# Query weight and half of the key weight loaded as float32 and cast by VectorE, with the prologue in a new order

## The chip, the cores and the metric

The kernel runs on all 8 cores of one Trainium2 chip. Each core works on its own 4,096 tokens, and no core waits for another. The metric is the device time of one execution in microseconds, that of the slowest core. Engines are named as in the profile: PE is TensorE (matrix products), PEld its weight loads, DVE is VectorE, ACT is ScalarE, POOL is GpSimd, and SP is SyncE, which only issues transfers (SPq).

## The reference

The input is x, 2 sequences of 16,384 tokens with 1,024 features. One layer is computed:

```
xn  = layernorm(x)
q, k, v = xn @ w_q + b_q, xn @ w_k + b_k, xn @ w_v + b_v      # 16 heads of 64
att = softmax over the 7 neighbouring tokens of q.k / 8, times v
t   = clip(round(w_ffn / s), -1, 1) * s,  s = max(mean |w_ffn|, 1e-5)
out = x + (att @ w_o + b_o) + xn @ t.T
```

All five weights are 1,024 x 1,024 in float32. The matrix products are made in bfloat16.

## The kernel before

A core reads its rows of x in 33 tiles of 128 tokens. Tokens are further grouped in 34 windows of 122 queries and 128 keys, and four windows make a block. A block of transposed, normalised inputs lies in one of three buffers `xnt`. The output comes in 32 tiles of 128 tokens.

A program in Python writes out, by hand and in order, one list of instructions for each engine (`Queues`). `q.do` appends an instruction, `q.dma` a transfer, and `q.need` a wait for a named result. Each engine works through its list strictly in order, so an instruction that waits holds up everything behind it on that engine. Transfers that SyncE issues go through one queue and follow each other there; GpSimd's go through another, and the two share the 16 DMA engines.

Each x tile goes through these steps: `x_load` (SyncE), `stats` (VectorE), `rstd` (two small instructions on ScalarE, a logarithm and an exponential), `normalise` (VectorE), and then a transpose. In the prologue (tiles 0 to 7, blocks 0 and 1) TensorE transposes and ScalarE copies the result (`xn_by_pe`); later a DMA does it (`xn_by_dma`).

A job on TensorE (`q_job`, `k_job`, `v_job`) is eight matmuls into one of three banks of `p_p`. ScalarE empties the bank (in the main loop VectorE does so for k), and a fourth job has to wait until the first bank is empty. `q_job(b, c)` and `k_job(b, c)` make 128 of the 1,024 output columns for block b, and c below 4 needs half 0 of the weight, the rest half 1.

For each window i and each half hf of the heads there follow: `scores` (TensorE), `mask_max` (VectorE: the mask addition, which frees the scores' bank, and then the row maximum), `exps` (ScalarE), `weights` (VectorE: reciprocal and product), `e_transpose` (a DMA), `att_v` (TensorE) and `att_evict` (ScalarE).

The feed-forward weight `wft` is loaded as float32 into memory that is otherwise used later (`wf_load`: the buffers of xr, the third xnt, et, att). VectorE sums the absolute values of its eight pieces (`wf_abs`); `wf_scale` forms the scale with one small matmul; `wf_tern` makes a ternary piece with two VectorE instructions, and all eight are wanted by the first feed-forward product.

The four attention weights are loaded by GpSimd and cast to bfloat16 on the way (`weight_load`): one transfer for 512 rows of a half, 1 MB read and 512 KB written. Waits in the lists of GpSimd and SyncE ("gates") set when they start:

- half 0 of wq in two pieces, after tiles 1 and 2 of x have landed
- x tile 4, behind half 0 of wq, in SyncE's list, and the tiles 5 to 7 behind it
- half 1 of wq and both halves of wk after tile 6 of x
- the eight pieces of wft after half 0 of wk, and x tiles 8 to 10 behind them
- wv and wo after the sixth piece of wft

The order of TensorE's jobs in the prologue is: q of block 0, c 0 to 3; q of block 1, c 0 to 3; the other q jobs; k of block 0, c 0 to 7; scores of window 0, half 0; two k jobs of block 1; `wf_scale`; scores of half 1; the other k jobs; v of window 0. Then the main loop begins: step s computes the scores and v of window s + 1 and finishes window s. In steps 4 and on it also makes the q and k jobs of the next block.

Of the kernel before, what the change touches and what calls it, by code (L numbers as in the profile page):

```python
# [91 lines left out]
def build_program():  # L92
# [13 lines left out]
    slots = (["cm", "cb", "ci", "bo"] + [f"{n}{k}" for n in ("wq", "wk", "wv", "wo") for k in range(2)] + [f"x{k}" for k in range(5)] + [f"r{k}" for k in range(NR)]  # L106
# [3 lines left out]
    with contextlib.ExitStack() as st:  # L110
# [52 lines left out]
        def weight_load(n, half, parts=(0, 1)):  # L163
            cols = slice(512 * half, 512 * half + 512)
            for k in parts:
                q.dma("gpsimd", f"{n}{half}", lambda e, k=k: e.dma_start(
                    w_b[n][:, 4 * k * H:(4 * k + 4) * H].rearrange("p (c n) -> p c n", c=4, n=H)[:, :, cols],
                    w_h[n][512 * k:512 * k + 512, cols].rearrange("(c p) n -> p c n", c=4, p=128)),
                    ("w", n, half))
# [109 lines left out]
        def q_job(b, c):  # L279
            n, bank = next_bank()  # L280
            m = TQ * nwin(b)
            q.need("tensor", ("w", "wq", c // 4), *[("xnt", b, r) for r in tiles_of(b)])
# [14 lines left out]
        def k_job(b, c, by="vector"):  # L297
            n, bank = next_bank()
            m = TQ * nwin(b) + KW - TQ
            q.need("tensor", ("w", "wk", c // 4), *[("xnt", b, r) for r in tiles_of(b)])  # L300
# [21 lines left out]
        def v_job(i, jh):  # L322
            b, w = divmod(i, BW)
            n, bank = next_bank()
            q.need("tensor", ("w", "wv", jh), *[("xnt", b, r) for r in tiles_of(b)])
# [131 lines left out]
        def o_proj(t):  # L457
            i = out_step(t)
            acc = p_out(t)
            q.need("tensor", ("w", "wo", 0), ("w", "wo", 1), ("att", i, 0))  # L460
# [67 lines left out]
        def wf_tern(j, k):  # L528
            up = w_b["wft"][:, k * H:(k + 1) * H]
            dn = brow[:, 512 * (j % 2):512 * (j % 2) + 512].bitcast(BF16)  # L530
            q.need("vector", "wthr")
# [9 lines left out]
        def bias_half(jh):  # L541
            n, bank = next_bank()
            q.need("tensor", ("w", "wo", jh), "bvb")
# [21 lines left out]
        q.need("gpsimd", ("x", 1))  # L565
        weight_load("wq", 0, (0,))
        q.need("gpsimd", ("x", 2))
        weight_load("wq", 0, (1,))
        q.need("sync", ("w", "wq", 0))
# [9 lines left out]
        bias_forms()  # L579
        normalise(3)  # L580
        for r in (5, 6, 7):
            x_load(r)
        q.need("gpsimd", ("x", 6))
        weight_load("wq", 1)
        weight_load("wk", 0)
        weight_load("wk", 1)
        xn_by_pe(3, 0, 1)
        for c in range(4):
            q_job(0, c)
            if c >= 1:  # L590
                stats(3 + c)
                rstd(3 + c)
                normalise(3 + c)
            if c >= 2:
                xn_by_pe(2 + c, 1)
        stats(7)
        rstd(7)
        normalise(7)
        xn_by_pe(6, 1)
        xn_by_pe(7, 1)  # L600
        q.need("sync", ("w", "wk", 0))
# [17 lines left out]
        for b, c in ([(1, c) for c in range(4)] + [(0, c) for c in range(4, 8)]  # L619
                     + [(1, c) for c in range(4, 8)]):  # L620
            q_job(b, c)
        for c in range(8):
            k_job(0, c, "scalar")
        scores(0, 0)
        mask_max(0, 0)
        k_job(1, 0, "scalar")
        k_job(1, 1, "scalar")
        wf_scale()
        some_terns(0, 2)
        scores(0, 1)  # L630
        mask_max(0, 1)
        some_terns(2, 4)
        for c in range(2, 8):
            k_job(1, c, "scalar")
            exps(0, (c - 2) // 3, ((0, 1), (2, 3, 4), (5, 6, 7))[(c - 2) % 3])
            if c == 5:
                weights(0, 0)
                some_terns(4, 6)
# [4 lines left out]
        weights(0, 1)  # L643
# [186 lines left out]
```

How the kernel before makes its waits and increments, by code:

```python
        def run(e, items):  # L754
            for f, sem, n in items:
                if f is None:
                    e.wait_ge(sems[sem], n)
                elif sem is None:
                    f(e)
                else:
                    f(e).then_inc(sems[sem], n)
```

## Time and profile before

| | |
|---|---|
| time, median of 3 runs | 695.19 us (694.86 to 695.31) |
| the profiled execution's own time | 696.35 us |
| its span, first to last instruction, slowest core (5) | 694.8 us |
| spans of the eight cores | 688.6 to 694.8 us |
| PE busy | 644.1 us, 93% |
| DVE busy | 434.4 us, 63% |
| ACT busy | 375.5 us, 54% |
| POOL busy | 88.6 us, 13% |

Busy time says how much work an engine has, not what sets the end. Views that show order are of more use here: the chain of waits follows the work that ended last back through what released each step; the timeline lists instructions with the idle time ahead of them and what ended it; the windows give busy time, the granted TensorE clock (1.00 is 2.4 GHz, 0.50 is 1.2 GHz) and the DMA engines' busy share for one stretch. All rows are of core 5.

### The profile page before, as it was taken

To read this page: it belongs to the slowest core of one execution; us is meant where nothing else is said; L and a number is where in the kernel's file an instruction comes from. 1 tells how busy PE (TensorE), PEld (TensorE's weight loads), DVE (VectorE), ACT (ScalarE), POOL (GpSimd) and SP (SyncE) were. 2 spreads that over 40 slices of the span, in tenths; PEclk is the share of its full clock that TensorE was granted. 3 is DMA by queue.
4 is the path that set the end of the run, shared out by engine and by line. 5 is a ranking of instruction groups with operands and counts; after the bars stand their busy time and mean duration, and the time that the engine had idled before them with its cause. 6 is when DMAs were issued, how large, how long until landed. Compare 5 with 4: busy or idle time off the path is not lost.

```text
span 694.8 us, 11677 instructions; the slowest of 8 cores (688.6 to 694.8 us)
## 1 busy us (share of the span) xinstructions
PE 644.1 (93%) x3890; PEld 299.8 (43%) x3890; DVE 434.4 (63%) x534; ACT 375.5 (54%) x1418; POOL 88.6 (13%) x52
## 2 busy tenths in 40 slices
PE   1669983999999999999999999999899999999996
PEld 1234431444444444444444444444344444455542
DVE  6225398686666667666665666666666755466663
ACT  3333465475555565656555555556556555555572
POOL 1202000221111111111111010011011111111110
PEclk9969996899999999999999999999999999999999
DMA  7699973768554444557563654544353442334423
GB/s 167 158 158 323 166 124 84 213 166 230 137 135 104 120 132 123 110 130 144 131 139 88 152 137 137 137 109 126 86 127 94 109 76 81 92 102 126 123 62 92
DMA packets 129947, 91.19 MB, mean 131 GB/s; under 512 B 107872, under 2 KB 116192, under 8 KB 129888
## 3 DMA queue, kind: packets, MB, share of 16 engines
q1 hardware_dynamic: 121440, 82.05, 45.9%
q0 software_dynamic: 8448, 8.39, 8.8%
q8 instruction: 32, 0.52, 0.3%
q14 instruction: 27, 0.22, 0.1%
HBM read 55.82 MB, written 16.78 MB: 104 GB/s over the span
## 4 chain that ended last, share of the span: by engine, by line
PE 83%; DVE 6%; DMA 4%; ACT 3%; issue 3%; DVEq 0%; SPq 0%; POOL 0%; ACTq 0%; POOLq 0%
PE p_p L284 16%; PE p_f L452 15%; PE p_p L302 15%; PE p_f L468 15%; PE p_p L327 15%; PE p_a L415 3%; PE p_s L355 3%; ACT sm L385 2%; DMA wq_b<-wq 1%; DVE sm L370 1%; DMA x<-x 1%; DMA sm<-x 1%; DVE bst L205 1%; DVE brow L534 1%; DVE wft_b L537 1%
## 5 line engine op out<-in xcount | busy, mean ns | idle before, releaser
L385 ACT ACTIVATE sm<-sm,nmx 122x128 f32<-122x128 f32 x544 | 210.9, 389 | 14.4 <-DVE nmx L377 14.4
L481 POOL TENSOR_TENSOR xr<-xr,brow 128x1024 f32<-128x1024 f32 x32 | 76.0, 2376 | 515.8 <-DMA xr<-x 452.3
L284 PE MATMUL p_p<-xnt,wq_b 128*128 128x488 bf16 (+1 forms) x576 | 129.2, 373 | 3.8 <-DMA wq_b<-wq 2.6
L327 PE MATMUL p_p<-wv_b,xnt 128*128 128x512 bf16 x544 | 124.5, 382 | 0.0
L302 PE MATMUL p_p<-xnt,wk_b 128*128 128x494 bf16 (+1 forms) x576 | 123.2, 361 | 0.0
L292 ACT ACTIVATE qt<-p_p,bq 128x488 bf16<-128x488 f32 (+1 forms) x72 | 46.5, 646 | 139.5 <-PE p_p L284 139.5
L452 PE MATMUL p_f<-wft_b,xnt 128*128 128x512 bf16 x496 | 114.7, 385 | 0.7 <-DVE xr L486 0.7
L468 PE MATMUL p_f<-wo_b,att 128*128 128x512 bf16 x496 | 113.2, 379 | 0.7 <-ACT att L432 0.7
L370 DVE TENSOR_TENSOR sm<-p_s,mk_sb 122x1024 f32<-122x1024 f32 x68 | 82.9, 1220 | 43.5 <-PE p_s L355 43.4
L385 ACT ACTIVATION_READ_ACCUMULATOR sm<-sm,nmx 122x1 f32 x544 | 102.4, 188 | 0.0
L340 ACT CAST v<-p_p 128x512 bf16<-128x512 f32 x68 | 39.0, 575 | 104.7 <-PE p_p L327 104.7
L398 DVE TENSOR_TENSOR en<-sm,rec 122x1024 bf16<-122x1024 f32 x68 | 83.3, 1226 | 11.6 <-DVE rec L392 11.4
L377 DVE TENSOR_REDUCE nmx<-sm 122x8 f32<-122x1024 f32 x68 | 83.0, 1220 | 7.4 <-DVE sm L370 0.5
L313 DVE TENSOR_SCALAR kt<-p_p,bias_sb 128x494 bf16<-128x494 f32 (+1 forms) x56 | 38.9, 695 | 77.4 <-PE p_p L302 77.4
L284 PEld LDWEIGHTS p_p<-xnt,wq_b 128*128 128x128 bf16 x576 | 57.7, 101 | 66.2 <-issue 13.1
L302 PEld LDWEIGHTS p_p<-xnt,wk_b 128*128 128x128 bf16 x576 | 56.2, 98 | 56.7
L327 PEld LDWEIGHTS p_p<-wv_b,xnt 128*128 128x128 bf16 x544 | 50.8, 98 | 60.8 <-issue 1.8
L452 PEld LDWEIGHTS p_f<-wft_b,xnt 128*128 128x128 bf16 x496 | 46.6, 99 | 56.4 <-issue 4.1
L468 PEld LDWEIGHTS p_f<-wo_b,att 128*128 128x128 bf16 x496 | 45.0, 98 | 56.6 <-issue 6.1
L392 DVE RECIPROCAL rec<-den 122x8 f32<-122x8 f32 x68 | 13.1, 192 | 66.4 <-ACT sm L385 66.4
L432 ACT ACTIVATE att<-p_a,wab 128x488 bf16<-128x488 f32 (+16 forms) x98 | 48.5, 524 | 11.1 <-PE p_a L415 10.9
L205 DVE BATCH_NORM_STATS2 bst<-x 128x6 f32<-128x512 f32 x62 | 39.6, 680 | 4.1 <-DMA x<-x 4.1
(62 smaller groups left out, 279.2 us busy)
## 6 DMA issues: line engine op xcount, KB each, us to landing
xr<-x SPq DMA_DIRECT2D x32, 512.0 KB, 4.7
x<-x SPq DMA_DIRECT2D x31, 512.0 KB, 4.5
out<-xr SPq DMA_DIRECT2D x31, 512.0 KB, 3.3
wq_b<-wq POOLq DMA_DIRECT2D x4, 512.0 KB, 9.1
wk_b<-wk POOLq DMA_DIRECT2D x4, 512.0 KB, 16.8
xr<-wft SPq DMA_DIRECT2D x4, 512.0 KB, 9.6
wv_b<-wv POOLq DMA_DIRECT2D x4, 512.0 KB, 16.0
wo_b<-wo POOLq DMA_DIRECT2D x4, 512.0 KB, 24.8
```

Of the source, the lines that this page charges most:

```text
L205: q.do("vector", lambda e, k=k: e.bn_stats(bs[:, 6 * k:6 * k + 6], xs[:, 512 * k:512 * k + 512]), ("bst", r, k))
L284: q.do("tensor", lambda e, k=k: e.matmul(bank[:, 0:m], w_b["wq"][:, k * H + 128 * c:k * H + 128 * c + 128], rows_of(b, k, BQ * b + 3, m), ...
L302: q.do("tensor", lambda e, k=k: e.matmul(bank[:, 0:m], w_b["wk"][:, k * H + 128 * c:k * H + 128 * c + 128], rows_of(b, k, BQ * b, m), star ...
L327: q.do("tensor", lambda e, k=k: e.matmul(bank, rows_of(b, k, TQ * i, KW), w_b["wv"][:, k * H + 512 * jh:k * H + 512 * jh + 512], start=(k ...
L370: q.do("vector", lambda e: e.tensor_tensor(heads(sm[hf]), heads(p_s), mk[0:TQ, KW * mt:KW * mt + KW][:, None, :].broadcast_to([TQ, 8, KW]) ...
L377: q.do("vector", lambda e: e.tensor_reduce(nmx[hf][0:TQ, :], heads(sm[hf]), AX.X, ALU.max, negate=True), ("nmx", i, hf))
L385: q.do("scalar", lambda e, h=h: e.activation(sm[hf][0:TQ, KW * h:KW * h + KW], sm[hf][0:TQ, KW * h:KW * h + KW], AF.Exp, bias=nmx[hf][0:TQ ...
L398: q.do("vector", lambda e: e.tensor_tensor(heads(en[hf]), heads(sm[hf]), rec[hf][0:TQ, :][:, :, None].broadcast_to([TQ, 8, KW]), ALU.mult) ...
L432: q.do("scalar", lambda e, done=done, at=at, m=m: e.activation(att[:, :].rearrange("p (c n) -> p c n", c=8, n=AR)[:, 4 * hf:4 * hf + 4, at ...
L452: q.do("tensor", lambda e, k=k, jh=jh: e.matmul(acc[:, 512 * jh:512 * jh + 512], rows_of(b, k, KW * t + 3, KW), w_b["wft"][:, k * H + 512 ...
L468: q.do("tensor", lambda e, k=k, jh=jh, lo=lo: e.matmul(acc[:, 512 * jh:512 * jh + 512], att[:, lo:lo + KW], w_b["wo"][:, k * H + 512 * jh: ...
L481: q.do("gpsimd", lambda e: e.tensor_tensor(xr[t % NR][:, :], xr[t % NR][:, :], brow[:, :], ALU.add), ("xrb", t))
```

## The change

The whole query weight and half 0 of the key weight are no longer cast on the way. They are loaded as float32 by SyncE, in pieces of 256 rows of a half (512 KB each, in runs of 2 KB), in line with the x tiles, into memory that belongs to the bfloat16 feed-forward and output weights, and VectorE casts each piece (`half_load`, `half_cast`). Half 1 of wk, wv and wo are still loaded by GpSimd. The gates are new: half 1 of wk starts after the second piece of half 0 of wk, wv after the sixth piece of wft, wo after that and after the casts of wq, from whose memory the output weight takes over. `x_load(4)` follows both halves of wq.

The prologue is put in another order. All eight q jobs of block 0 come first, then those of block 1; the statistics and rstd of tile 8 move from the first step of the main loop to a place ahead of all k jobs; scores of window 0 come after four k jobs of each half; `wf_scale` and the ternaries come later in the lists, and the ternaries follow `weights` of window 0.

```diff
+        stage = [w_b[n][:, 2 * H * k:2 * H * k + 2 * H].bitcast(F32)
+                 for n in ("wft", "wo") for k in range(4)]
+        staged = {("wq", 0): 0, ("wq", 1): 4, ("wk", 0): 0}
+        def weight(n, half):
+            if (n, half) in staged:
+                return [("cast", n, half, k) for k in range(4)]
+            return [("w", n, half, k) for k in range(2)]
+        def half_load(n, half):
+            for k in range(4):
+                j = staged[(n, half)] + k
+                if (n, half) == ("wk", 0):
+                    q.need("sync", ("cast", "wq", 0, k))
+                q.dma("sync", f"h{j}", lambda e, k=k, j=j: e.dma_start(
+                    stage[j].rearrange("p (c n) -> p c n", c=2, n=512),
+                    w_h[n][256 * k:256 * k + 256, 512 * half:512 * half + 512]
+                    .rearrange("(c p) n -> p c n", c=2, p=128)), ("h", n, half, k))
+        def half_cast(n, half, k):
+            j = staged[(n, half)] + k
+            q.need("vector", ("h", n, half, k))
+            q.do("vector", lambda e: e.tensor_copy(
+                w_b[n][:, 2 * k * H:(2 * k + 2) * H].rearrange("p (c n) -> p c n", c=2, n=H)[
+                    :, :, 512 * half:512 * half + 512],
+                stage[j].rearrange("p (c n) -> p c n", c=2, n=512)), ("cast", n, half, k))
...
-            q.need("vector", "wthr")
+            q.need("vector", "wthr", *weight("wk", 0))
...
-        q.need("gpsimd", ("x", 1))
-        weight_load("wq", 0, (0,))
-        q.need("gpsimd", ("x", 2))
-        weight_load("wq", 0, (1,))
-        q.need("sync", ("w", "wq", 0))
+        half_load("wq", 0)
+        half_load("wq", 1)
         x_load(4)
...
-        bias_forms()
+        half_cast("wq", 0, 0)
         normalise(3)
+        xn_by_pe(3, 0, 1)
         for r in (5, 6, 7):
             x_load(r)
-        q.need("gpsimd", ("x", 6))
-        weight_load("wq", 1)
-        weight_load("wk", 0)
+        for k in range(1, 4):
+            half_cast("wq", 0, k)
+        bias_forms()
+        for k in range(4):
+            half_cast("wq", 1, k)
+        half_load("wk", 0)
+        q.need("gpsimd", ("h", "wk", 0, 1))
         weight_load("wk", 1)
-        xn_by_pe(3, 0, 1)
-        for c in range(4):
-            q_job(0, c)
-            if c >= 1:
-                stats(3 + c)
-                rstd(3 + c)
-                normalise(3 + c)
-            if c >= 2:
-                xn_by_pe(2 + c, 1)
-        stats(7)
-        rstd(7)
-        normalise(7)
-        xn_by_pe(6, 1)
-        xn_by_pe(7, 1)
-        q.need("sync", ("w", "wk", 0))
         for k in range(8):
             wf_load(k)
         q.need("gpsimd", ("wf", 5))
         weight_load("wv", 0)
         weight_load("wv", 1)
+        q.need("gpsimd", *weight("wq", 1))
         weight_load("wo", 0)
         weight_load("wo", 1)
+        for c in range(8):
+            q_job(0, c)
+            if c >= 4:
+                stats(c)
+                rstd(c)
+                if c >= 5:
+                    normalise(c - 1)
+                if c >= 6:
+                    xn_by_pe(c - 2, 1)
+        normalise(7)
         for r in range(8, 8 + NX):
             x_load(r)
+        xn_by_pe(6, 1)
+        xn_by_pe(7, 1)
+        for k in range(4):
+            half_cast("wk", 0, k)
+        for c in range(8):
+            q_job(1, c)
         for k in range(8):
             wf_abs(k, "vector")
+        stats(8)
+        rstd(8)
+        for c in range(4):
+            k_job(0, c, "scalar")
+        scores(0, 0)
+        mask_max(0, 0)
+        for c in range(4):
+            k_job(1, c, "scalar")
+            if c >= 1:
+                exps(0, 0, ((0, 1), (2, 3, 4), (5, 6, 7))[c - 1])
+        for c in range(4, 8):
+            k_job(0, c, "scalar")
+        scores(0, 1)
+        mask_max(0, 1)
+        k_job(1, 4, "scalar")
+        wf_scale()
...
+        weights(0, 0)
+        some_terns(0, 4)
+        for c in range(5, 8):
             k_job(1, c, "scalar")
+            exps(0, 1, ((0, 1), (2, 3, 4), (5, 6, 7))[c - 5])
+        weights(0, 1)
+        some_terns(4, 6)
         v_job(0, 0)
         v_evict(0, 0)
         v_job(0, 1)
         v_evict(0, 1)
-        weights(0, 1)
...
             if r is not None:
-                if s == 0:
-                    stats(r)
-                    rstd(r)
                 normalise(r)
```

## Rows read from the trace of the kernel before

**Rows 1.** The chain of waits, 0 to 140 us: start, length, what.
```profile
21.14 6.71 DMA sm<-x
...
30.02 0.30 ACT mv L218
...
43.93 22.46 PE p_p L284 x96
66.40 13.33 PE p_p L302 x64
```

**Rows 2.** Timeline of VectorE: start, length, line, operation, tiles [idle before].
```profile
16.00 0.69 DVE L187 CAST bvb<-bias_sb 128x1024 bf16<-128x1024 f32 x1
...
40.61 0.81 DVE L226 TENSOR_SCALAR xn<-x,mv 128x1024 bf16<-128x1024 f32 x1 [1.25 <-ACT mv L218]
56.23 1.22 DVE L504 TENSOR_REDUCE wab<-xr 128x1 f32<-128x1024 f32 x1 [14.81 <-DMA xr<-wft]
...
67.89 1.22 DVE L504 TENSOR_REDUCE wab<-att 128x1 f32<-128x1024 f32 x1 [0.48 <-DMA att<-wft]
80.24 1.23 DVE L370 TENSOR_TENSOR sm<-p_s,mk_sb 122x1024 f32<-122x1024 f32 x1 [11.13 <-PE p_s L355]
...
84.63 0.75 DVE L534 TENSOR_SCALAR brow<-et,wab 128x1024 bf16<-128x1024 f32 x1
...
102.30 1.22 DVE L370 TENSOR_TENSOR sm<-p_s,mk_sb 122x1024 f32<-122x1024 f32 x1
...
107.22 1.28 DVE L205 BATCH_NORM_STATS2 bst<-x 128x6 f32<-128x512 f32 x2
...
113.33 0.20 DVE L392 RECIPROCAL rec<-den 122x8 f32<-122x8 f32 x1 [1.32 <-ACT sm L385]
...
120.47 1.22 DVE L370 TENSOR_TENSOR sm<-p_s,mk_sb 122x1024 f32<-122x1024 f32 x1
```

**Rows 3.** Windows: stretch, busy time of each engine, PEclk, DMA share, GB/s.
```profile
12.00:34.00 22.00, 13.27 (x70) 6.86 (x68) 9.24 (x19) 9.44 (x17) 3.11 (x5) 0.95 0.70 145
34.00:69.00 35.00, 28.52 (x138) 13.45 (x137) 14.66 (x17) 13.85 (x22) 5.58 (x8) 0.83 1.09 237
45.00:50.00 5.00, 5.00 (x16) 1.94 (x15) 0.00 (x0) 0.71 (x2) 0.00 (x0) 0.60 1.14 151
```

**Rows 4.** Timeline of TensorE, its matmuls.
```profile
21.41 6.91 PE L284 MATMUL p_p<-xnt,wq_b 128*128 128x488 bf16 x24 [2.59 <-DMA wq_b<-wq]
...
103.67 0.61 PE L355 MATMUL p_s<-kt,qt 64*128 64x128 bf16 x8 [2.27 <-DVE sm L370]
...
121.83 0.61 PE L355 MATMUL p_s<-kt,qt 64*128 64x128 bf16 x8 [5.63 <-DVE sm L370]
```

**Rows 5.** Timeline of ScalarE, the rstd of x tile 8.
```profile
108.90 0.30 ACT L215 ACTIVATE mv<-mv,cst 128x1 f32<-128x1 f32 x1 [6.83 <-DVE mv L210]
```

**Rows 6.** Transfers by tile: masks, x7, first half of wk, x8; issue, then landing.
```profile
L173 SPq DMA_DIRECT2D mk_sb<-mk x1: 1087/1087/1087, 4.1 to 4.1; - x1
...
DMA to landing us min/median/max: 8.1/8.1/8.1
...
L198 SPq DMA_DIRECT2D x<-x x1: 1487/1487/1487, 22.5 to 22.5; - x1
...
DMA to landing us min/median/max: 9.2/9.2/9.2
...
L166 POOL DMA_DIRECT2D wk_b<-wk x2: 760/765/770, 32.4 to 33.1; - x2
...
DMA to landing us min/median/max: 12.7/14.1/15.5
...
L198 SPq DMA_DIRECT2D x<-x x1: 380/380/380, 54.1 to 54.1; - x1
...
DMA to landing us min/median/max: 15.2/15.2/15.2
```

**Rows 7.** The page's DMA issues: count, KB each, median us to landing.
```profile
x<-x SPq DMA_DIRECT2D x31, 512.0 KB, 4.5
```

More of the change, by code:

```diff
@@ L105, in build_program @@
     tile_of = {out_step(t): t for t in range(NO)}
-    slots = (["cm", "cb", "ci", "bo"] + [f"{n}{k}" for n in ("wq", "wk", "wv", "wo") for k in range(2)] + [f"x{k}" for k in range(5)] + [f"r{k}" for k in range(NR)]
+    slots = (["cm", "cb", "ci", "bo"] + [f"{n}{k}{j}" for n in ("wk", "wv", "wo") for k in range(2) for j in range(2)]
+             + [f"h{k}" for k in range(8)] + [f"x{k}" for k in range(5)] + [f"r{k}" for k in range(NR)]
              + [f"o{k}" for k in range(NR)] + [f"t{k}{j}" for k in range(3) for j in range(RT)] + [f"te{k}" for k in range(2)]
@@ L165, in weight_load @@
             for k in parts:
-                q.dma("gpsimd", f"{n}{half}", lambda e, k=k: e.dma_start(
+                q.dma("gpsimd", f"{n}{half}{k}", lambda e, k=k: e.dma_start(
                     w_b[n][:, 4 * k * H:(4 * k + 4) * H].rearrange("p (c n) -> p c n", c=4, n=H)[:, :, cols],
                     w_h[n][512 * k:512 * k + 512, cols].rearrange("(c p) n -> p c n", c=4, p=128)),
-                    ("w", n, half))
+                    ("w", n, half, k))
+        stage = [w_b[n][:, 2 * H * k:2 * H * k + 2 * H].bitcast(F32)
[21 more added lines that the diff above has]
+                stage[j].rearrange("p (c n) -> p c n", c=2, n=512)), ("cast", n, half, k))
         def constant_load():
@@ L281, in q_job @@
             m = TQ * nwin(b)
-            q.need("tensor", ("w", "wq", c // 4), *[("xnt", b, r) for r in tiles_of(b)])
+            q.need("tensor", *weight("wq", c // 4), *[("xnt", b, r) for r in tiles_of(b)])
             for k in range(8):
@@ L299, in k_job @@
             m = TQ * nwin(b) + KW - TQ
-            q.need("tensor", ("w", "wk", c // 4), *[("xnt", b, r) for r in tiles_of(b)])
+            q.need("tensor", *weight("wk", c // 4), *[("xnt", b, r) for r in tiles_of(b)])
             for k in range(8):
@@ L324, in v_job @@
             n, bank = next_bank()
-            q.need("tensor", ("w", "wv", jh), *[("xnt", b, r) for r in tiles_of(b)])
+            q.need("tensor", *weight("wv", jh), *[("xnt", b, r) for r in tiles_of(b)])
             for k in range(8):
@@ L459, in o_proj @@
             acc = p_out(t)
-            q.need("tensor", ("w", "wo", 0), ("w", "wo", 1), ("att", i, 0))
+            q.need("tensor", *weight("wo", 0), *weight("wo", 1), ("att", i, 0))
             order = [(k, jh) for k in range(8) for jh in range(2)]
@@ L542, in bias_half @@
             n, bank = next_bank()
-            q.need("tensor", ("w", "wo", jh), "bvb")
+            q.need("tensor", *weight("wo", jh), "bvb")
             for k in range(8):
@@ L617, in some_terns @@
                 wf_tern(j, k)
[L619 to L633, printed above, removed]
+        weights(0, 0)
+        some_terns(0, 4)
+        for c in range(5, 8):
             k_job(1, c, "scalar")
[L635 to L638, printed above, removed]
+            exps(0, 1, ((0, 1), (2, 3, 4), (5, 6, 7))[c - 5])
+        weights(0, 1)
+        some_terns(4, 6)
         v_job(0, 0)
```

## The prediction

> **What bounds the kernel now.** I read the page first: TensorE is busy 93% of the span, and the slices show its holes only at the left edge, in the first 125 us. So the change, which touches only the work ahead of the main loop, is worth what it does to those holes. The chain of waits [rows 1] shows the first: the last input tile that the first q jobs need, x4, lands at 21.14 + 6.71 = 27.85 us. The SyncE queue holds it until half of the query weight is in, and block 1 can only be normalised after it: the last of its tiles is done at 41.4 [rows 2]. The long run of q jobs starts at 43.93, with four of sixteen done, and its 96 matmuls take 22.46 us. At the rate of the key matmuls behind them (13.33 us for 64, 0.208 each) they would take 20.0; the other 2.5 us are a start at the half clock, which the windows show: granted 0.60 (16 matmuls) in 45 to 50 us, after TensorE had sat with little to do [rows 1, 3].
>
> The second hole is in VectorE's hands. From 84.63, where the ternary weight starts, to 120.47 VectorE goes from one instruction to the next, and TensorE waits for it twice: the scores at 103.67 and those at 121.83 are both released by VectorE's mask addition, which reads "sm L370" [rows 2, 4]. Inside it ScalarE loses 6.83 us at 108.90: the rstd of tile 8 stands in its queue ahead of the attention eviction and the exponentials, and VectorE reaches the statistics of tile 8 only at 107.22 [rows 2, 5]. From 121.83 on TensorE is nearly always busy, so the result is read at the mask addition that begins at 120.47: what moves it, moves the end by as much.
>
> **The first weights.** The tables and masks, the last transfer ahead of the weights, land at 4.1 + 8.1 = 12.2 us [rows 6]. Behind them the same queue now carries float32 pieces of 512 KB: 8 of wq, x4 to x7, 4 of wk, 8 of the feed-forward weight, x8: 25 pieces in line. No row shows a float32 piece in runs of 2 KB. From below: x5 to x7 landed between 27.85 and 22.5 + 9.2 = 31.7, 1.28 us each [rows 1, 6]. From above: the casting transfer moves the same 2 KB reads, and its two pieces land at 32.4 + 12.7 = 45.1 and 33.1 + 15.5 = 48.6 us, 3.5 us for 1 MB, or 1.75 for 512 KB [rows 6]. In between, the eight feed-forward pieces were summed by VectorE as they landed, seven intervals in 11.66 us, 1.67 each, while a cast shared the engines [rows 2]. I take 1.6, near that longest run.
>
> The Trainium skill (HBM Reference, "Specifications (TRN2)") gives a core about 358 GB/s when both cores of a pair stream. That would be an estimate of 1.46 us for a piece; the run above is slower and the three x tiles are faster, so the rows decide. By it x8 below would land at 56.0 and the kernel would end at 686.1; nothing else here uses it.
>
> So wq half 0 lands at 12.2 + 4 x 1.6 = 18.6 and half 1 at 25.0, x4 to x7 at 26.6 to 31.4. The eight casts cost VectorE at most 0.75 us each (the cast of 128x1024 that stands there takes 0.69 [rows 2]); VectorE idles there now, from its last normalisation of block 0 to x4. The first half is cast at 19.4. The first q job waits longer for the transpose copies of tile 3, and starts at 20.0 instead of 21.41 [rows 4], which alone is worth nothing. All eight q jobs of block 0 then run while x4 to x7 arrive: 64 x 0.208 + 2.5 of half clock = 15.8, until 35.8. Block 1 is normalised from 26.7 at about 2.3 us a tile (statistics 1.6, normalisation 0.7), until 36.4; transposes and copies follow, and q of block 1 starts at 38.7 with eight jobs done. It ends at 38.7 + 13.3 = 52.0, where it ended at 66.40 before [rows 1]. The moved biases (0.9 us) and the memory that pieces borrow from other weights cost nothing: those weights come later.
>
> **The new wait.** The statistics and rstd of tile 8 are now ahead of the key jobs. That puts rstd(8) in ScalarE's queue before the evictions of the key jobs, and stats(8) in VectorE's behind all eight wf sums. TensorE has three banks: it runs k jobs 0 to 2, 5.0 us, until 57.0, and must then wait for ScalarE, which waits for x8, the 25th piece. That x8 lands at 12.2 + 25 x 1.6 + 6.9 (the two casting pieces of the second key half, which share the engines) + 0.4 (the first value piece) = 59.5. From landing to the end of rstd takes 2.5 us (x4: 27.85 to 30.32 [rows 1]) and the eviction of the first key job 0.7, so the fourth key job starts at 62.7: a hole of 5.7 us, and the half clock again, 2.5. A second way to x8: the DMA share was 0.70 over 12 to 34 us and 1.09 over 34 to 69 [rows 3], so 22 x 0.39 / 1.09 = 7.9 us of engine time lay idle; x8 landed at 54.1 + 15.2 = 69.3 [rows 6]; less 7.9, less 6 x 3.5 - 12 x 1.6 = 1.8 for float32 in place of casts, is 59.6.
>
> From 62.7 TensorE has nine key jobs and the first scores until the second scores: 9 x 8 x 0.208 + 0.3 + 2.5 = 17.8, so 80.5, and the mask addition behind them starts at 81.1.
>
> **VectorE's chain.** Before, the mask addition at 80.24 led to the first ternary at 84.63, 4.4 us, part of it waiting for a key job; I take 4.2: 85.3. From 84.63 to 102.30 VectorE did six ternaries, two weights and one mask and maximum pair, 17.67 us; the pair (102.30 to 107.22 holds two, 4.92) is now ahead: 17.67 - 2.46 = 15.2 [rows 2]. So the mask addition of 102.30 comes at 100.5, only 1.8 us earlier. Behind it, two pairs 4.9, normalise(8) 0.8 without its statistics (1.6) and without the wait for ScalarE, stats(9) 1.6: 107.8. The exponentials are ready by then, since rstd(8) no longer stands ahead of them: scores at 101.8, eviction by 103.5, eight exponentials 3.1, 106.6. The rest took 113.33 to 120.47, 7.14 us, and is the same work [rows 2]. That gives 114.9, against 120.47: 5.6 us earlier. The removal of stats(8) from this place is worth most of it: 1.6 + 0.9 + 1.3 of waiting [rows 2, 5].
>
> **Hidden at no price.** The value weight starts when the sixth wf piece lands, about 55, and its four pieces with x8 to x10 need 4 x 3.5 + 3 x 1.6 = 19: in by 78, wanted at 89. The output weight follows by 92, wanted after 110. If that cover went, each microsecond late would be one of TensorE. The three banks, the main loop and the tail are untouched.
>
> **The sum.** The profiled execution took 696.35 us around a span of 694.8; the median of the runs is 695.19. 695.2 - 5.6 = **689.6 us**.
>
> **Rivals.** *No hole at rstd(8).* If x8 lands by 57.0 - 3.2 = 53.8, or 1.37 us a piece, the key jobs run through: 5.7 + 2.5 more, a gain of about 14, 681. If TensorE falls to half clock in its gap at 36 to 38.7, 683.9. For it: three pieces at 1.28; the queue is never empty now. Against: the run of eight at 1.67, the casts that share it. At 1.45 x8 lands at 55.8, a hole of 2 us is left, and the time is 686.
>
> *The wait eats the gain.* The gain is 65.1 minus the landing of x8. At 1.75 a piece x8 lands at 63.2 and 693.3 is left; between 63.7 and 66.5 it cannot be told from no change. For it: both ends of the bracket, and that the slowest of eight cores counts.
>
> *Slower.* The price of a piece goes by the DMA and not by its bytes: a float32 piece of 2 KB runs costs what a casting piece costs, 3.5 us. Then x8 lands at 12.2 + 12 x 3.5 + 13 x 1.6 + 7.3 = 82.3, ScalarE stands until 85, and the kernel ends near 712. It decides from 2.2 us a piece on (x8 at 66.5). For it: nothing shows such a piece. Against: bytes explain the 1.67 and the 3.5 alike.
>
> *A fixed part for each DMA, paid in turn.* The x loads, most of them alone in their queue, take 4.5 us from issue to landing in the median [rows 7]; were each of the twelve new pieces to pay that before the next, x8 would land at 12.2 + 12 x 4.5 + 13 x 1.6 + 7.3 = 94.3 and the end would be 724. Against: seven intervals of 1.67 in one queue [rows 2]. The Trainium skill (DMA: Bandwidth & Descriptors, "Rules for kernel authors") asks for 1 MiB or more in a DMA, and its "Anatomy of one DMA" puts a fixed 2.0 us on each; here pieces are halved, so the rule speaks against this change, but the trace shows the fixed part overlapped.
>
> **Chances.** Forecast, a gain of 2 to 9: 0.62. No hole, or nearly none, over 9: 0.18. Eaten: 0.10. Slower by piece price 0.07, by a fixed part 0.03. The runs of this kernel tell 0.2%, 1.4 us, from no change; so faster 0.80, same 0.10, slower 0.10. The range takes in most of the no-hole cases and stops at the first that are eaten: 683 to 694.
>
> **What the profile would show.** Right: the first q matmul near 20, q of block 0 without a break, q of block 1 from about 39; a TensorE hole after 24 key matmuls at 57, ended by ScalarE's eviction, with ScalarE waiting for VectorE's rstd input and VectorE for x8; the fourth key job at 60 to 66; the mask additions of 102.30 and 120.47 at about 100.5 and 115; no ScalarE wait of 6.8 us at rstd. Wrong, if float32 pieces land more than 1.75 us or less than 1.4 us apart; if TensorE waits for wq's casts; if the main loop, once TensorE is full, keeps another pace.

## The result, and the profile after

The changed kernel takes 699.38 us (median of 4 runs, 697.82 to 700.67), the kernel before beside it 695.25 (694.86 to 695.54). The ratio is 1.0057, with an interval of 1.0043 to 1.007: it is 0.6% slower, where the prediction said 689.6 and a gain. Here and below, times are medians over executions in which nothing disturbed a die. The profiled execution took 700.67 us; its slowest core is now core 3, with a span of 699.0 us. Rows of after are of core 3 unless a core is named, and lines of the kernel have moved by some 30 (L370 of before is L400).

The chain of waits (start, length, what) answers to [rows 1]:

```profile
16.20 16.59 DMA x<-x
...
38.80 25.89 DMA x<-x
...
64.78 1.30 DVE bst L235 x2
...
66.48 0.31 ACT mv L245
...
67.07 0.66 ACT kt L346
...
67.87 3.46 PE p_p L332 x8
...
72.84 15.23 PE p_p L332 x64
...
88.15 0.68 ACT kt L346
...
108.74 1.23 DVE sm L400
...
123.37 1.23 DVE sm L400
```

The long q run is gone from it. In its place stands the transfer of x tile 8, on its way from 38.80 to 64.69 us, and then the path that the prediction named: statistics, rstd, the eviction of a key job, the fourth key job. The transfer by itself, by tile, answers to the last lines of [rows 6]:

```profile
L228 SPq DMA_DIRECT2D x<-x x1: 422/422/422, 38.8 to 38.8; - x1
...
DMA to landing us min/median/max: 25.9/25.9/25.9
```

TensorE's timeline (start, length, line, operation, count [idle before and what ended it]) answers to [rows 4]:

```profile
21.07 13.75 PE L314 MATMUL p_p<-xnt,wq_b 128*128 128x488 bf16 x56 [2.74 <-DVE bq L216]
...
42.98 14.70 PE L314 MATMUL p_p<-xnt,wq_b 128*128 128x488 bf16 x64 [1.25 <-ACT xnt L292]
57.52 5.16 PE L332 MATMUL p_p<-xnt,wk_b 128*128 128x494 bf16 x24
67.87 3.45 PE L332 MATMUL p_p<-xnt,wk_b 128*128 128x494 bf16 x8 [5.19 <-ACT kt L346]
72.23 0.61 PE L385 MATMUL p_s<-kt,qt 64*128 64x128 bf16 x8 [0.92 <-ACT kt L346]
72.78 15.28 PE L332 MATMUL p_p<-xnt,wk_b 128*128 128x494 bf16 x64
89.08 0.40 PE L385 MATMUL p_s<-kt,qt 64*128 64x128 bf16 x8 [1.02 <-ACT kt L346]
```

There is the forecast hole, after 24 key matmuls and ended by ScalarE's eviction, but five microseconds late. Behind it the first 8 matmuls take 3.45 us and the next 64 take 15.28, where 64 took 13.33 in [rows 1]; and twice the scores wait for the eviction of the key job right ahead of them, 0.92 and 1.02 us. The windows show the half clock (columns as in [rows 3]):

```profile
42.00:92.00 50.00, 41.15 (x184) 17.84 (x184) 17.85 (x18) 18.05 (x40) 5.99 (x9) 0.86 1.03 196
65.00:70.00 5.00, 2.13 (x6) 0.86 (x7) 1.28 (x3) 2.28 (x5) 0.00 (x0) 0.62 1.19 177
70.00:75.00 5.00, 4.08 (x18) 1.44 (x17) 1.87 (x2) 0.67 (x1) 0.00 (x0) 0.50 1.16 158
75.00:80.00 5.00, 5.00 (x23) 2.14 (x21) 0.57 (x1) 2.29 (x7) 0.00 (x0) 0.86 1.14 154
```

The granted clock is 0.62, 0.50 and 0.86 after TensorE has stood still from 62.7 to 67.9. ScalarE's timeline has the rstd of [rows 5] at its new place; the evictions of all three banks stand behind it:

```profile
66.48 0.30 ACT L245 ACTIVATE mv<-mv,cst 128x1 f32<-128x1 f32 x1 [8.03 <-DVE mv L240]
66.87 0.30 ACT L248 ACTIVATE mv<-mv,cst 128x1 f32<-128x1 f32 x1
67.07 1.78 ACT L346 ACTIVATE kt<-p_p,bias_sb 128x494 bf16<-128x494 f32 x3
```

VectorE's timeline answers to [rows 2]:

```profile
26.41 0.69 DVE L196 CAST wq_b<-wo_b 128x1024 bf16<-128x1024 f32 x1 [0.51 <-DMA wo_b<-wq]
28.38 0.69 DVE L196 CAST wq_b<-wo_b 128x1024 bf16<-128x1024 f32 x1 [1.28 <-DMA wo_b<-wq]
...
64.78 1.28 DVE L235 BATCH_NORM_STATS2 bst<-x 128x6 f32<-128x512 f32 x2 [1.44 <-DMA x<-x]
73.02 1.23 DVE L400 TENSOR_TENSOR sm<-p_s,mk_sb 122x1024 f32<-122x1024 f32 x1 [6.64 <-PE p_s L385]
89.59 1.23 DVE L400 TENSOR_TENSOR sm<-p_s,mk_sb 122x1024 f32<-122x1024 f32 x1 [14.01 <-PE p_s L385]
94.97 0.75 DVE L564 TENSOR_SCALAR brow<-et,wab 128x1024 bf16<-128x1024 f32 x1
...
97.03 0.75 DVE L564 TENSOR_SCALAR brow<-att,wab 128x1024 bf16<-128x1024 f32 x1
...
108.74 1.22 DVE L400 TENSOR_TENSOR sm<-p_s,mk_sb 122x1024 f32<-122x1024 f32 x1
...
123.37 1.22 DVE L400 TENSOR_TENSOR sm<-p_s,mk_sb 122x1024 f32<-122x1024 f32 x1
```

VectorE idles 6.64 and 14.01 us until the two scores come, and only then begins the work that before ran from 84.63 on. The mask addition that the result was to be read at starts at 123.37.

### The profile page after: what moved, and what is told of

It is laid out like the page before. It is cut to its first block, busy times and chain, and to the rows that moved or that the text cites. A ratio compares the mean times of both kernels' runs of the same rounds, so it can differ in the third digit from the quotient of the medians.

```text
span 699.0 us, 11726 instructions; the slowest of 8 cores (694.7 to 699.0 us)
## 1 busy us (share of the span) xinstructions
PE 648.8 (93%) x3890; PEld 300.1 (43%) x3890; DVE 445.3 (64%) x546; ACT 376.1 (54%) x1418; POOL 83.2 (12%) x46
## 4 chain that ended last, share of the span: by engine, by line
PE 80%; DMA 7%; DVE 6%; issue 2%; ACT 2%; SPq 2%; DVEq 0%; ACTq 0%
PE p_p L332 15%; PE p_f L482 15%; PE p_f L498 15%; PE p_p L357 15%; PE p_p L314 13%; DMA x<-x 6%; PE p_a L445 3%; PE p_s L385 3%; ACT sm L415 2%; SPq L188 1%; DVE sm L400 1%; DVE wft_b L567 1%; DVE bst L235 1%; DVE brow L564 1%; DVE en L428 1%
## 5 line engine op out<-in xcount | busy, mean ns | idle before, releaser
L332 PE MATMUL p_p<-xnt,wk_b 128*128 128x494 bf16 (+1 forms) x576 | 128.0, 370 | 5.2 <-ACT kt L346 5.2
L314 PE MATMUL p_p<-xnt,wq_b 128*128 128x488 bf16 (+1 forms) x576 | 127.1, 369 | 4.0 <-DVE bq L216 2.7
L400 DVE TENSOR_TENSOR sm<-p_s,mk_sb 122x1024 f32<-122x1024 f32 x68 | 83.0, 1220 | 53.0 <-PE p_s L385 51.5
L415 ACT ACTIVATION_READ_ACCUMULATOR sm<-sm,nmx 122x1 f32 x544 | 105.2, 193 | 0.0
L370 ACT CAST v<-p_p 128x512 bf16<-128x512 f32 x68 | 39.1, 577 | 104.6 <-PE p_p L357 104.6
L428 DVE TENSOR_TENSOR en<-sm,rec 122x1024 bf16<-122x1024 f32 x68 | 85.7, 1260 | 12.0 <-DVE rec L422 11.8
L482 PEld LDWEIGHTS p_f<-wft_b,xnt 128*128 128x128 bf16 x496 | 46.7, 99 | 56.4 <-issue 4.2
```

The source lines that it names most:

```text
L314: q.do("tensor", lambda e, k=k: e.matmul(bank[:, 0:m], w_b["wq"][:, k * H + 128 * c:k * H + 128 * c + 128], rows_of(b, k, BQ * b + 3, m), ...
L332: q.do("tensor", lambda e, k=k: e.matmul(bank[:, 0:m], w_b["wk"][:, k * H + 128 * c:k * H + 128 * c + 128], rows_of(b, k, BQ * b, m), star ...
L400: q.do("vector", lambda e: e.tensor_tensor(heads(sm[hf]), heads(p_s), mk[0:TQ, KW * mt:KW * mt + KW][:, None, :].broadcast_to([TQ, 8, KW]) ...
L415: q.do("scalar", lambda e, h=h: e.activation(sm[hf][0:TQ, KW * h:KW * h + KW], sm[hf][0:TQ, KW * h:KW * h + KW], AF.Exp, bias=nmx[hf][0:TQ ...
L428: q.do("vector", lambda e: e.tensor_tensor(heads(en[hf]), heads(sm[hf]), rec[hf][0:TQ, :][:, :, None].broadcast_to([TQ, 8, KW]), ALU.mult) ...
L482: q.do("tensor", lambda e, k=k, jh=jh: e.matmul(acc[:, 512 * jh:512 * jh + 512], rows_of(b, k, KW * t + 3, KW), w_b["wft"][:, k * H + 512 ...
```

## The experiments

Five stations, read from the timelines and averaged over the eight cores, put all kernels beside each other: the first key job, the fourth key job, the mask addition of the second scores, and the mask additions of windows 1 and 2 (in core 3 above: 57.52, 67.87, 89.59, 108.74, 123.37). Stations and landings are those of one profiled execution of each kernel, which lies up to 2.1 us off the kernel's median. Times in us; the ratio is to the kernel before on the same chip.

| kernel | x8 lands | key 1 | key 4 | second scores | window 1 | window 2 | time | ratio (interval) |
|---|---|---|---|---|---|---|---|---|
| before | 66.1 | 63.1 | 68.1 | 85.6 | 99.2 | 117.3 | 695.25 | |
| changed | 64.3 | 56.4 | 67.5 | 88.8 | 107.9 | 122.5 | 699.38 | 1.0057 (1.0043-1.007) |
| e6 loads alone | 63.5 | 67.5 | 72.5 | 90.1 | 103.6 | 121.9 | 700.62 | 1.008 (1.006-1.0101) |
| e4 order alone | 65.2 | 65.7 | 70.7 | 88.8 | 108.0 | 122.2 | 703.24 | 1.0118 (1.01-1.0135) |
| e1 rstd behind | 63.5 | 55.4 | 60.4 | 78.6 | 97.7 | 112.3 | 690.86 | 0.9929 (0.9912-0.9945) |
| e2 x8 ahead | 43.0 | 56.3 | 61.3 | 79.4 | 98.6 | 113.2 | 692.06 | 0.9943 (0.9923-0.9963) |
| e3 old place | 63.5 | 56.1 | 61.1 | 79.2 | 98.3 | 116.8 | 695.50 | 0.9994 (0.9983-1.0005) |
| e5 ternaries early | 63.5 | 56.2 | 66.6 | 87.3 | 101.6 | 115.8 | 695.65 | 1.0004 (0.999-1.0018) |
| e7 both | 63.9 | 56.2 | 61.2 | 80.0 | 90.6 | 106.4 | 684.69 | 0.9849 (0.9826-0.9871) |
| e8 both and more | 64.0 | 55.9 | 60.9 | 80.1 | 89.5 | 104.1 | 680.43 | 0.9786 (0.9769-0.9803) |
| e9 nothing behind | 63.4 | 55.9 | 66.6 | 88.3 | 107.4 | 122.0 | 698.92 | 1.0047 (1.002-1.0075) |
| e10 casts behind | 56.5 | 55.7 | 60.7 | 78.9 | 98.0 | 112.6 | 690.81, two runs | none |
| e11 whole rows | 61.0 | 62.1 | 67.1 | 85.2 | 104.4 | 119.0 | 697.26, one run | none |
| e12 stats alone | 65.6 | 62.7 | 67.7 | 85.2 | 98.8 | 113.0 | 692.08 | 0.9948 (0.9932-0.9964) |
| e13 one cast behind | 60.5 | 56.4 | 63.6 | 82.6 | 101.8 | 116.4 | 694.07 | 0.9972 (0.9962-0.9983) |

The theories were: the hole at rstd(8) and what it pushes back (H); the loads themselves, which come too late for the first jobs (L); VectorE's work, which is put behind the second scores and left in one piece there (V); and, later, the depth of the queues behind x8 (D).

**The hole.** Is it the place of rstd(8), or the loads?

```diff
-        stats(8)
-        rstd(8)
         for c in range(4):
             k_job(0, c, "scalar")
         scores(0, 0)
         mask_max(0, 0)
+        stats(8)
...
+        rstd(8)
         for c in range(4, 8):
             k_job(0, c, "scalar")
```

> The changed kernel with stats(8) behind the first mask_max of window 0 and rstd(8) behind the key jobs of block 1 (c 0 to 3), so that no eviction of a key job stands behind it in ScalarE's queue. Theory H (the hole: x8 lands late and reaches TensorE through rstd(8) in ScalarE's queue): the fourth key job starts at about 61 instead of 67 to 68, without the half clock; the second scores come some 9 to 10 us earlier, and with them VectorE's ternaries and the end: 690. Theory L (the float32 stream is the price, everything lands later): x8 still lands at 64, the first mask addition waits for the sums instead, and the time stays at 698 to 700. Theory V (the ternaries start too late in VectorE's list) gives the same gain as H here, since they follow the second scores.

Measured: 690.86 us. x8 lands as late as before the edit, and TensorE runs its 32 key matmuls without a break (core 5, TensorE's timeline):

```profile
56.74 6.83 PE L332 MATMUL p_p<-xnt,wk_b 128*128 128x494 bf16 x32
64.49 0.40 PE L385 MATMUL p_s<-kt,qt 64*128 64x128 bf16 x8 [0.91 <-ACT kt L346]
64.82 13.51 PE L332 MATMUL p_p<-xnt,wk_b 128*128 128x494 bf16 x64
79.35 0.40 PE L385 MATMUL p_s<-kt,qt 64*128 64x128 bf16 x8 [1.02 <-ACT kt L346]
```

Moving two statistics instructions and one rstd behind other work is worth 8.5 us (9.0 in the mean span, 696.1 to 687.1). The 64 matmuls take 13.51 rather than 15.28: the half clock goes with the hole. The two waits of the scores, 0.91 and 1.02, stay. So H holds: with the very same loads the kernel is now 4.9 us faster than before, and L can't explain the loss of the changed kernel. The other way round, the place is kept and x8 comes early:

```diff
+        x_load(8)
         for k in range(8):
             wf_load(k)
...
+        stats(8)
+        rstd(8)
         for k in range(8):
             wf_abs(k, "vector")
-        stats(8)
-        rstd(8)
```

> The changed kernel with x tile 8 loaded ahead of the eight pieces of the feed-forward weight, and stats(8) ahead of their sums; rstd(8) stays ahead of the key jobs. Theory H: it is the late x8 that opens the hole and not the place of rstd(8) by itself, so the hole closes here too: x8 lands near 46, key jobs run through, 690 to 691 (the sums end one piece later). Theory L: one piece more ahead of the feed-forward weight, 699 to 701.

692.06 us, x8 at 43.0 (46 was expected), no hole. Two ways to take the wait away give nearly one time, so it was the wait and not the place as such. The place matters in another way: e3 puts both back into the first step of the main loop, where the kernel before had them.

```diff
-        stats(8)
-        rstd(8)
...
+                if s == 0:
+                    stats(r)
+                    rstd(r)
```

> The changed kernel with stats(8) and rstd(8) back in the first step of the main loop, as before the change. Theory H: the hole closes (9 to 10 us), but the wait in the first step is back (statistics 1.6, the wait for rstd 0.9, late exponentials 1.3): 693 to 694. Theory L: no hole is of account, only the wait comes back: 702 to 703.

695.50 us, 1.5 above what was expected. There is no hole (key job 4 at 61.1), but from window 1 to window 2 it takes 18.5 us instead of 14.6. The old place costs 4.6 against e1. The next kernel asks the same of the other side, the kernel before with this one thing changed:

```diff
+        stats(8)
         scores(0, 0)
         mask_max(0, 0)
+        rstd(8)
...
-                if s == 0:
-                    stats(r)
-                    rstd(r)
```

> The kernel before with only stats(8) and rstd(8) taken out of the first step of the main loop: stats(8) ahead of the first mask addition, where VectorE idles, rstd(8) behind the last key eviction of block 0. By the prediction's account of that place (1.6 + 0.9 + 1.3 = 3.8 us): 691 to 692. If the step is bound elsewhere: 695.

692.08 us. With the old loads and the old order this edit alone gives 3.8 us (695.89 beside it), and window 2 comes 4.3 earlier: the prediction's 3.8 for this part was right. It also puts the rest of the change in its place: e1, the whole change without its hole, gives 4.9, so the new loads and the new order together add about 1 us to what this one move gives in the kernel before, less than the intervals of the two ratios can tell apart.

**Loads and order apart.** e6 has the new loads in the old order; e4 has the new order with the old casting loads and gates. The main part of e4's edit:

```diff
-        half_load("wq", 0)
-        half_load("wq", 1)
+        q.need("gpsimd", ("x", 1))
+        weight_load("wq", 0, (0,))
+        q.need("gpsimd", ("x", 2))
+        weight_load("wq", 0, (1,))
+        q.need("sync", *weight("wq", 0))
...
```

> The loads of the change (float32 pieces, casts, gates) with the order of jobs, ternaries and statistics of the kernel before. Theory L: x4 lands at 30 instead of 24 (mean of the cores), and in this order TensorE's long run of q jobs waits for block 1, so everything behind comes 5 to 6 us later: 700 to 701, that is, the loads alone explain the loss. Theory H: the loads cost little here, since no key job waits for x8: 695 to 697.

> The order of the change with the casting loads and the gates of the kernel before. The second half of the query weight then lands near 39 to 41, so that the q jobs 4 to 7 of block 0 wait for it, key jobs begin at 62 and the fourth waits for rstd(8), x8 landing at 66: a hole of 2 to 3 us. Theory H: 700 to 702, the order alone is no gain either. Theory L: without the float32 stream the order gains what was forecast, 689 to 691.

700.62 and 703.24: each part alone loses more than both together. e6 is what theory L expected of it: x4 lands at 29.3 (24.2 before), block 1 waits for it with only four of the sixteen q jobs done, and the key jobs begin 4.4 late. That is the price of the loads in the old order; in the new one, e1 has them and gains. e4 lies above the 700 to 702 that was expected of it: its key jobs begin 2.6 late, not 1 early, and the hole of 2 to 3 us isn't there (5.0 us from key job 1 to 4 on every core). The stations divide the change. From the first key job to window 2 it is 54.2 us before, 54.4 with the loads alone, 56.5 with the order alone, 56.9 in e1, and 66.1 in the changed kernel. So the two parts together bring the key jobs 6.7 us forward, the order takes back 2.3 to 2.7 (with what the new place of stats(8) gives already in it), and the hole with its half clock takes 9.2: +5.2 in sum, and the mean span grew by 4.7 (691.4 to 696.1).

**VectorE's idle time.** In e5 the hole stays, and four ternaries move up into VectorE's idle stretch behind the first scores.

```diff
         scores(0, 0)
+        wf_scale()
         mask_max(0, 0)
+        some_terns(0, 4)
...
         weights(0, 0)
-        some_terns(0, 4)
```

> The changed kernel with the scale and the first four ternaries right behind the first scores, where VectorE stands idle for 14 us, instead of behind the second mask addition; stats(8) and rstd(8) stay, and so does the hole. Theory V: the mask addition of window 1 comes at about 100 instead of 108, and the end with it: 691 to 692. Theory H alone: the end hangs on the hole, nothing is gained: 698 to 700.

695.65 us: between the theories. From the second scores to window 1 it is 14.3 us instead of 19.1, so 4.8 less and not 8.2 for four ternaries at 2.06 each (94.97 to 97.03 above). VectorE's timeline (core 5) shows where the rest stays:

```profile
89.40 1.22 DVE L400 TENSOR_TENSOR sm<-p_s,mk_sb 122x1024 f32<-122x1024 f32 x1 [4.91 <-PE p_s L385]
...
98.13 0.20 DVE L422 RECIPROCAL rec<-den 122x8 f32<-122x8 f32 x1 [4.74 <-ACT sm L415]
...
103.68 1.22 DVE L400 TENSOR_TENSOR sm<-p_s,mk_sb 122x1024 f32<-122x1024 f32 x1
```

It now waits 4.74 us for ScalarE's exponentials, with two ternaries left behind that wait. e7 is e1 and e5 together, with those two put ahead of it, and e8 adds one key job between eviction and scores and moves one more ternary ahead. e8's edit against the changed kernel, in part:

```diff
+        k_job(1, 0, "scalar")
         scores(0, 0)
+        wf_scale()
         mask_max(0, 0)
+        stats(8)
+        some_terns(0, 5)
...
+        rstd(8)
...
+        k_job(1, 4, "scalar")
         scores(0, 1)
         mask_max(0, 1)
-        k_job(1, 4, "scalar")
-        wf_scale()
...
```

> e1_rstd_behind with the scale and four ternaries right behind the first scores and two more behind the first weights of window 0. Theories H and V each hold a part, and the parts add: the mask addition of window 1 comes at about 90 instead of 98, the end at 683 to 684. If V is only another way round the same hole, it adds nothing here: 690 to 691.

> e7_both with one key job between the eviction that the scores wait for and the scores, in both halves (two waits of 0.9 to 1.0 us), and with one more ternary early, so that one instead of two is left in the first step. If the waits count and VectorE still bounds the first step: 3 to 4 us below e7_both, near 680. If TensorE or ScalarE bounds it by now: no better than e7_both.

684.69 and 680.43 us. e8 beats both kernels, by 2.1% the one before. How its 4.3 us over e7 divide between the key jobs and the ternary was not tried. In it TensorE has no gap from 42 to 92 us (windows, core 4), and the scores no longer wait for the eviction (TensorE's timeline):

```profile
42.00:92.00 50.00, 49.95 (x253) 22.83 (x254) 35.66 (x43) 23.83 (x61) 5.95 (x9) 0.97 1.12 207
```

```profile
56.67 8.50 PE L332 MATMUL p_p<-xnt,wk_b 128*128 128x494 bf16 x40
65.10 0.40 PE L385 MATMUL p_s<-kt,qt 64*128 64x128 bf16 x8
```

**Why x8 is late.** First the depth: does what is queued behind x8 slow it?

```diff
+        x_load(8)
+        q.need("gpsimd", ("x", 8))
+        weight_load("wv", 0)
...
+        q.need("sync", ("x", 8))
+        for r in range(9, 8 + NX):
```

> The changed kernel with nothing in flight behind x8: x tiles 9 and 10 and the value weight are issued only when x8 has landed. Theory D (depth: in a long line the 16 engines run ahead of each other, and a tile has landed only when the slowest has done its share, so x8 pays for bytes that stand behind it): x8 lands near 61 instead of 64.3 (mean of the cores), and the time falls with it to 696 to 697. Theory R (rate alone: each piece takes 1.9 us): x8 still lands at 64, 699 to 700.

No: x8 lands at 63.4, where e1, e3 and e5, which have the loads of the changed kernel as they are, have it at 63.5; the time is 698.92, within the runs of the changed kernel. D falls. Then what shares the engines with the line: e10 starts the casting half of wk only behind the last wf piece.

```diff
-        q.need("gpsimd", ("h", "wk", 0, 1))
-        weight_load("wk", 1)
...
+        x_load(8)
+        q.need("gpsimd", ("wf", 7))
+        weight_load("wk", 1)
...
```

> The changed kernel with the casting load of the second key half issued only after the last feed-forward piece, so that it no longer shares the engines with the line ahead of x8. By the prediction's term for the two casts, 6.9 us, x8 lands near 57.4 instead of 64.3, the hole at the fourth key job shrinks to nothing, and the time falls to 690 to 691, as in e1_rstd_behind. If the casts cost the line nothing (they fill gaps), x8 stays at 64 and the time at 699.

x8 lands at 56.5, 7.8 us earlier, and the hole is gone; two executions took 690.64 and 690.97. In the part that is not shown the edit also puts the value weight behind x8, as e9 does; against e9 the casts alone make 6.9 us (63.4 to 56.5). The eight wf pieces then land 1.56 us apart (44.0 to 55.0, mean of the cores). VectorE's timeline (core 6) shows the statistics of tile 8 begin nine microseconds ahead of those above:

```profile
53.90 1.22 DVE L534 TENSOR_REDUCE wab<-att 128x1 f32<-128x1024 f32 x1
55.52 1.29 DVE L235 BATCH_NORM_STATS2 bst<-x 128x6 f32<-128x512 f32 x2 [0.40 <-DMA x<-x]
```

Then the pieces: e11 loads wq in eight pieces of 128 whole rows, so in runs of 4 KB and the same 512 KB each.

```diff
+                if n == "wq":
+                    q.dma("sync", f"h{j}", lambda e, j=j: e.dma_start(
+                        stage[j], w_h["wq"][128 * j:128 * j + 128, :]), ("h", n, half, k))
+                    continue
...
```

> The changed kernel with the query weight in eight pieces of 128 whole rows (runs of 4 KB as in the x tiles, the same 512 KB each) instead of runs of 2 KB. All eight must then be there for the first q job, so only the landings are of interest. If the short runs are what makes the pieces slow: eight pieces in 12.8 us, the last near 25.4. If every piece in a full line takes that long: near 28, as in the changed kernel.

They take 1.62 us each, the last lands at 25.8; in runs of 2 KB it was 1.89 each and 28.0. VectorE's casts (core 1) go by this step:

```profile
20.99 0.69 DVE L203 CAST wq_b<-wo_b 128x1024 bf16<-128x1024 f32 x1 [0.29 <-DMA wo_b<-wq]
22.91 0.69 DVE L203 CAST wq_b<-wo_b 128x1024 bf16<-128x1024 f32 x1 [1.23 <-DMA wo_b<-wq]
24.19 0.69 DVE L203 CAST wq_b<-wo_b 128x1024 bf16<-128x1024 f32 x1 [0.58 <-DMA wo_b<-wq]
25.63 0.69 DVE L203 CAST wq_b<-wo_b 128x1024 bf16<-128x1024 f32 x1 [0.75 <-DMA wo_b<-wq]
```

The kernel gains little by it, since every q job now needs all eight pieces and the first starts at 27.0. Last, x8 nearly where it was forecast:

```diff
-        weight_load("wk", 1)
+        weight_load("wk", 1, (0,))
...
+        q.need("gpsimd", ("wf", 7))
+        weight_load("wk", 1, (1,))
...
```

> The changed kernel with one of the two casting pieces of the second key half behind the last feed-forward piece, the other at its place: a step half way to e10_cast_behind. By the measured price of the two (6 to 8 us) x8 lands at 60.4 to 61.3, which is nearly where the prediction had put it. If the end follows x8 one for one while a hole is left, and the prediction failed only in the landing, the time is 689.6 to 691, as forecast for x8 at 59.5; if the stretch from the hole to the second scores also costs more than was counted (21.2 instead of 17.8 us), the fourth key job starts near 64 and the time is 695 to 697.

694.07 us, just under the second of the two, but not for its reason. With x8 at 60.5 instead of 64.3 the fourth key job starts at 63.6, and from there to the mask addition of the second scores it takes 19.0 us in the mean, where the prediction had 18.4 and the changed kernel took 21.3. The hole is 2.79 us on the slowest core (7) and shorter on others (core 1 below it; TensorE's timelines):

```profile
55.91 5.16 PE L332 MATMUL p_p<-xnt,wk_b 128*128 128x494 bf16 x24
63.87 3.03 PE L332 MATMUL p_p<-xnt,wk_b 128*128 128x494 bf16 x8 [2.79 <-ACT kt L346]
67.82 0.61 PE L385 MATMUL p_s<-kt,qt 64*128 64x128 bf16 x8 [0.91 <-ACT kt L346]
68.36 14.87 PE L332 MATMUL p_p<-xnt,wk_b 128*128 128x494 bf16 x64
```

```profile
63.26 1.83 PE L332 MATMUL p_p<-xnt,wk_b 128*128 128x494 bf16 x8 [1.97 <-ACT kt L346]
...
66.33 13.51 PE L332 MATMUL p_p<-xnt,wk_b 128*128 128x494 bf16 x64
```

On four cores the holes are 0.59 to 1.97 us and the stretch takes 18.1, as in e1, without the half clock; on the other four they are 2.79 to 3.18 and it takes 19.5 to 20.9. So behind x8 the path runs nearly as forecast: from 60.5 on, the prediction's own terms put the second scores at 82.1 and window 2 at 115.9, and they stand at 82.6 and 116.4. Still the kernel is only 1.9 us faster than before (695.93 beside it), not the 4.6 that the prediction's line leaves for this landing (65.1 - 60.5). So the landing of x8 is only part of the miss; most of what is missing here lies in the base that the gain was counted from (below).

## Why the prediction was wrong

The mechanism was right and three sizes were off. By the profiled executions the forecast was 696.35 - 5.6 = 690.75, and 700.67 came: 9.9 us. In core 3, x8 makes 5.2 (64.69 for 59.5), the stretch from the fourth key job to the second mask addition 3.3 (67.87 to 89.59 is 21.7; 62.7 to 81.1 was forecast, 18.4), and the main loop 1.3 (575.6 us from window 2 to the end of the span, 574.3 in core 5 before). In the mean of the cores x8 makes 4.8 and the stretch 2.9 (21.3), so that window 2 comes 7.6 late (122.5 for 114.9); the main loop took no longer there, and the other 2 of the 9.9 us are the base below. VectorE's chain makes nothing: 19.15 and 14.63 for 19.4 and 14.4.

**The first weights: the step that failed.** "I take 1.6, near that longest run" was too low for the new pieces. Over the cores, the terms of the landing of x8 came out so: tables and masks 12.9 for 12.2; eight wq pieces 15.1 for 12.8; x4 to x7 7.1 for 6.4; four wk pieces 8.0 for 6.4; wf with the casts 18.6 for 19.7; the value piece and x8 2.5 for 2.0. That is +4.8 us, 3.9 of it in the twelve new pieces, at 1.93 each. The upper bound of 1.75, beyond which the prediction called itself wrong, was too low: it came from a casting transfer, whose reads are in the same runs but which is another kind of transfer. e11 shows that for wq the form of the pieces is at fault, since the same bytes in whole rows take 1.62, as forecast (one execution, eight cores). The casts' 6.9 us held (without them, in e10, the wf pieces take 6.1 us less, and x8 lands 6.9 before that of e9).

The Trainium skill (DMA: Bandwidth & Descriptors, "Specifications") gives 512 B as the smallest transfer at line rate. The runs of 2 KB are well above it, and the trace does not speak against it: but for the two long intervals named below, the new pieces took 1.72 us each (1.62 in e10), the whole rows 1.62. The estimate of 1.46 us a piece by the 358 GB/s of the Trainium skill (HBM Reference, "Specifications (TRN2)") lies below every run of eight pieces here, 1.56 in e10 at the least; only x8 to x10 there came faster, 1.34 apart (55.0 to 59.0).

**The stretch behind the hole.** Two things were not in it. The scores need the key job right ahead of them, so TensorE waits for its eviction: 0.92 + 1.02 us, where in the order of before four and two other key jobs stood between. e8 puts one there, and the wait is gone. And the half clock cost 3.8 and not 2.5: 18.73 us for 72 matmuls that take 15.0 at 0.208 (in e13 15.34 in core 1 and 17.90 in core 7). The 2.5 came from a start after a thin stretch [rows 1, 3]; here TensorE had stood still for five.

**The base.** The gain was counted against one core. Core 5 reaches window 2 at 120.47 [rows 2], the other seven by 117.7 at the latest, 117.3 in the mean of all. Its x4 landed at 27.85 us, 24.2 in the mean. The forecast 114.9 was worked out mostly from rates that hold for any core, and against the mean it is 2.4 us and not 5.6. After the change the cores lie at 121.1 to 124.3. The experiments bear this out: window 2 of e1, e12 and e13 comes 5.0, 4.3 and 0.9 us earlier than the mean of before, 8.1, 7.5 and 4.1 earlier than core 5, and the times fell by 4.9, 3.8 and 1.9.

**What held.** The first q job (21.07 for 20.0, behind the moved biases and not behind the transposes), the nearly unbroken q of block 0 (one wait of 0.58 us), the hole and its chain of waits, VectorE's chain, the vanished wait of 6.83 us at rstd, and the main loop (from window 2 to the end of the span, mean of the cores, 574.1 before and 573.6 after). q of block 1 began at 42.98 for 38.7, for x4 landed 4.1 late (30.68); that alone cost nothing, as the hole was behind it.

**The rivals.** "The wait eats the gain" is the way it went, at 0.10. Its line, 65.1 minus the landing of x8, would still have left 0.4 to 0.8 us; the stretch and the base made a loss of it. "No hole", 681 by the prediction, gives 690.9 when it is made (e1): the key jobs begin at 55.4 and not at 52.0, the stretch behind the fourth takes 18.1 us and not 15.9 (18.4 less the half clock), and the rest is the base. The price of 3.5 us for each piece and the fixed part of 4.5 us are out: the pieces came 1.9 apart in one queue. The rule of the Trainium skill that asks for 1 MiB or more (DMA: Bandwidth & Descriptors, "Rules for kernel authors") warned in the right direction, but the size of the pieces was not the cause: 512 KB in whole rows took 1.62 us each, as forecast.

What stays open is why the new pieces are slower. Much of their excess sits in two intervals: the fifth wq piece took 3.1 us and the first wk piece 2.8, each the first of a half (the first of all, at 1.6, was not slow), while the other ten took 1.72. It is so in every kernel here that loads both weights in this form: 2.7 to 3.1 and 2.6 to 3.3, the other ten 1.58 to 1.72 in the mean. So the price of an ordinary piece was nearly right, and two late pieces make 2.8 of the 3.9 us. In e11, with whole rows of wq, the fifth wq piece took 1.5, but the first wk piece, still half a row wide, again came 3.1 us after x7. That the length of the runs does it is not shown; no kernel was made to tell this apart.

## What to carry to other kernels

When a small instruction is moved ahead in an in-order list, price what it waits for against everything that is then behind it: here two tiny ScalarE instructions held the evictions of three banks for the length of a queue of 25 transfers, and moving them was worth 8.5 us. Make the sum for all cores and not for the slowest alone, whose lateness may be its own and not part of the mechanism. Once a hole is gone, look for what idles ahead of the next wait: the ternaries in VectorE's idle time and one job between an eviction and its reader gave another 10 us. And try each part alone: the statistics and rstd of one tile, moved in the kernel before, gave 3.8 of the 4.9 us that the whole change gives without its hole.

## What the runs showed of the hardware

Behind a standstill of 5.19 us, matmuls that take 0.208 us each at full clock took 3.45 us for 8, and the granted clock was 0.62, 0.50 and 0.86 in the windows of 5 us from 65 to 80 us. Behind 1.97 us (e13, core 1) 8 took 1.83, and the granted clock was 1.00 in all windows of 5 us from 60 to 80 us; behind 2.79 (core 7) 8 took 3.03, and it was 0.50 from 65 to 70 us. Two casting transfers of 1 MB delayed the end of a line of transfers on another queue by 6.9 us (x8 in e9 and e10), where the 3.5 us between their landings in [rows 6] make 7.0 for the two. The times at which early transfers land differ by several microseconds between cores of one execution: x4 of the kernel before landed at 22.2 to 27.8.
